# RWKV-6 time mixing with a BitNet feed-forward: decay totals computed first, queries prepared a level ahead, small matmuls split over parts of the array, head variances with the means as stationary operand

## The chip, the cores and the metric

The kernel runs on one core of a Trainium2 chip. Time is device time in microseconds (us). Three runs of the kernel before have a median of 3308.46 us (3307.17 to 3309.01). Engines: PE is TensorE, DVE VectorE, ACT ScalarE, POOL GpSimd, SP SyncE; psP, psW, psX, psY, psF are PSUM tensors.

## The reference, cut to what matters

Input x is 4 x 2048 x 512. An RWKV-6 time mix (16 heads of 32 channels) is followed by a layer norm, a feed-forward with ternary weights (512 to 2048 to 512), and another layer norm:

```python
mix = jnp.tanh((x + xx * time_maa_x) @ maa_w1).reshape(b, t, 5, E_MIX)      # five mixes of rank 32
mix = jnp.einsum('btfe,fec->fbtc', mix, maa_w2); mw, mk, mv, mr, mg = mix
xw = x + xx * (time_maa_w + mw)                                             # and xk, xv, xr, xg likewise
r = xr @ Wr.T; k = xk @ Wk.T; v = xv @ Wv.T; g = jax.nn.silu(xg @ Wg.T)
w = time_decay + jnp.tanh(xw @ td_w1) @ td_w2
decay = jnp.exp(-jnp.exp(w))
def step(S, inp):
    kv = k_t[..., :, None] * v_t[..., None, :]
    y = jnp.einsum('bhk,bhkj->bhj', r_t, S + u[None, :, :, None] * kv)
    S = d_t[..., None] * S + kv
y = ((y - mu) / jnp.sqrt(var + EPS)).reshape(b, t, c) * ln_g + ln_b         # mean and variance per head
x = layernorm(x + (y * g) @ Wo.T)
x = layernorm(x + layernorm(gelu(x @ ternary(W_fc).T)) @ ternary(W_proj).T)
```

## The kernel before

**Tiles.** A tile is 64 time steps of all four batch rows, so 256 columns (`COLS`); `PAIRS` = 2 halves of 128 columns belong to two batch rows each. There are 32 tiles, one after the other, since the state S goes from tile to tile. In tile `it` the attention of tile `it` is interleaved by hand with the feed-forward of tile `it - 1` (`ffn.up`, `ffn.down`, `ffn.stats`, and `ffn.late`, which finishes the tile before that one). Tile 0 has no feed-forward; a last piece (`alone`) has no attention. Each engine runs its own instruction list in program order, and semaphores tie the lists together. `Ring` hands out PSUM banks in a fixed order: `wait_free` waits until the former content of a bank has been read.

**Scan by levels.** Inside a tile the recurrence is solved by doubling: blocks of 1, 2, 4, 8, 16 and 32 steps. `D` holds the decay of each step, `TOT[2n]` the product of decays over 2n steps. At each level DVE multiplies the right halves of the queries `RM` by the total of the left neighbour (`scale_right`, L1114), and the left halves of the keys `KM` by the total of the right neighbour (`scale_left`, L1126), and makes the next total (L1127). Then ACT (three heads of a group, L661) and DVE (the fourth, `queries`, L1102) copy the right query halves into one of two buffers `RB`, PE multiplies keys by queries (`l2`, `l4`, `l8`, `l16` in psW, L464; `l32` at L481), and DVE copies the blocks into `A` (`copy_predicated`, L1169). RM is scaled in place, so `scale_right` of a level waits for the copies of the level below. Between the levels PE runs one `ffn.down(0, i)` each. Before the levels DVE multiplies queries by u (L1138), and PE runs `l1_0` and `l1_1` (L447).

**Order on DVE in the levels.** After `ffn.up(0, 3)`: for n = 2, 4, 8, 16: `scale_right` and `queries` (n = 2 had its own ahead of the loop), `scale_left` with the next total, `copy_predicated`, and at n = 2 `ffn.fold(0, 0)` (L1296), a reduction of 1.0 us.

**After the levels.** ACT copies the blocks into AB (`matrices`), PE makes y (`from_state`, `from_chunk`, L506 and L518), DVE copies it to YSB, ACT squares it (L771). PE sums the squares per head (`var`, L564: eight matmuls with the squares as stationary operand and 4 columns of HEAD_MEAN moving), runs `up(1, 3)` and `down(1, 0)` to `down(1, 2)`. ACT takes square roots (L787) behind its part of `up(1, 3)`, DVE takes reciprocals (L1213) and spreads them over the head's channels (L1217), PE transposes them (`rb`, L577), DVE multiplies y by them, applies the affine map and the gate (L1223 to L1231), and PE runs `wo` (L591). Between `rb` and `wo` PE makes the arguments of the five tanh (`tanh_argument`, L359): `w1a` with 128 columns of stationary operand, `w1b` with 32, each over 256 moving columns. ACT takes their tanh (L792, L794), copies high parts (`mix_high`, L661), POOL the remainders (`mix_low`, L867).

**Start of a tile.** `mix` of "mk" (L375), `td1` (L402, 64 columns stationary), `ffn.late` (`down(before, 1, 3)`, L637), `mix` of "mv", `td2` (L412, 64 rows), `ffn.tokens` (L607), then the k channels (L393), `up(0, 0)` (L618), and so on. ACT takes the tanh of td1 (L684) and the exponentials of td2 (L694). DVE reads the feed-forward's sums in `moments` (L1306). In `F_SEQ` the product of the second half, `pj_1`, stands ahead of its sums, `st_1`, though PE issues the sums first; so `moments` waits for both.

Of the kernel before, what the change touches and what calls it, by code (L numbers as in the profile page):

```python
# [11 lines left out]
ALU = mybir.AluOpType  # L12
# [29 lines left out]
         ("r0", "act"), ("r1", "act"), ("g0", "dve"), ("g1", "dve"), ("var", "act"), ("rb0", "dve"), ("rb1", "dve"),  # L42
# [12 lines left out]
         for n, e in (("fc0", "act"), ("fc1", "act"), ("fc2", "act"), ("fc3", "act"), ("pj", "product"), ("st", "stats"))]  # L55

F_BANKS = [0, 1, 0, 1, 0, 1, 1, 0, 1, 0, 1, 0]
# [47 lines left out]
def rwkv_ffn_kernel(nc, x_ch, x_tok, w_all, w1, w2a, w2b, td1, td2, par, wfc, wpj, ffn_wb, c_f32, c_mask, out,  # L105
                    tiles=TILES):
    with ExitStack() as ctx:
# [11 lines left out]
        TD2 = sb("TD2", [DECR, C])[:, :]  # L119
# [12 lines left out]
        HEAD_MEAN = CF[:, o:o + HPG]; o += HPG  # L132
# [29 lines left out]
        TZ = sb("TZ", [DECR, COLS])[:, :]  # L162
# [61 lines left out]
        rs_inv, y_affine, z_ready = sem("rs_inv"), sem("y_affine"), sem("z_ready")  # L224
        bn_done, mv_ready, rstd_ready = sem("bn_done"), sem("mv_ready"), sem("rstd_ready")
# [37 lines left out]
        NWEIGHTS = 7 + 5 * 4  # L263
# [15 lines left out]
        def _(sp):  # L279
# [49 lines left out]
        def _(pe):  # L329
# [49 lines left out]
            pe.wait_ge(w2_split, 6)  # L379
            mix(-1, 0, "mw", lambda name: None)  # L380

            def tile(it, first, ffn):
# [18 lines left out]
                for k in range(KC):  # L401
                    mm = pe.matmul(psP[0:DECR, P.bank("td1"), 0:COLS], TD1[:, k, :], cc(XF[1], k),  # L402
                                   start=(k == 0), stop=(k == KC - 1))
# [5 lines left out]
                for g in range(2):  # L409
                    P.wait_free(pe, it, f"td2{g}", first)  # L410
                    for c in range(2):
                        mm = pe.matmul(psP[:, P.bank(f"td2{g}"), COLS * c:COLS * (c + 1)],  # L412
                                       TD2[:, 128 * (2 * g + c):128 * (2 * g + c + 1)], TZ[:, :], start=True, stop=True)
                    mm.then_inc(p_full, 1)
# [146 lines left out]
                for p in range(PAIRS):  # L561
                    for c in range(KC):
                        o = HEADS * p + HPG * c
                        mm = pe.matmul(psP[:, P.bank("var"), o:o + HPG], cc(YSQ, c)[:, 128 * p:128 * (p + 1)], HEAD_MEAN,  # L564
                                       start=True, stop=True, skip_group_check=True)
# [33 lines left out]
            def feed_forward(j, before):  # L599
# [41 lines left out]
                def alone():  # L641
                    late()
                    tokens()
                    for p in range(PAIRS):
                        for g in range(4):
                            up(p, g)
                        for part in range(4):
                            down(j, p, part)
                        stats(p)
# [9 lines left out]
        def _(act):  # L659
# [3 lines left out]
            def mix_high(t):  # L663

# [761 lines left out]
```

## Time and profile before

| | |
|---|---|
| median of three runs | 3308.46 us |
| the profiled execution | 3307.6 us, its span 3305.7 us |
| PE busy | 3080.0 us, 93% |
| PE weight load busy | 2229.9 us, 67% |
| DVE busy | 2449.2 us, 74% |
| ACT busy | 1913.6 us, 58% |
| POOL busy | 933.9 us, 28% |
| mean granted PE clock | 0.982 |

Shares are means over stages with different limits; busy time of a matmul is modelled with its end, and matmuls overlap. A row of the timeline gives start, duration, engine, line, operation, output and input, count, and in brackets the idle time of the engine before it with what ended it. A float32 matmul stands in two records.

### The profile page before, as it was taken

What the parts mean: (1) busy time and instruction counts of PE and PEld (TensorE: products, weight loads), DVE (VectorE), ACT (ScalarE), POOL (GpSimd) and SP (SyncE); (2) the same over time, 40 slices, a digit from 0 to 9 for tenths busy, and PEclk for the clock granted to TensorE, in tenths of its full rate; (3) what the DMA queues carried; (4) which work ended last, traced back from release to release, by engine and by line L of the source; (5) the groups of instructions that cost most, each with busy time, mean ns of one, the idle gap of its engine ahead of it and who ended that gap; (6) DMA issues with size and microseconds to landing.
All of it is one profiled execution on the core that took longest, in us unless ns stands there. A gap on an engine that the chain in (4) does not pass through costs nothing.

```text
span 3305.7 us, 98915 instructions
## 1 busy us (share of the span) xinstructions
PE 3080.0 (93%) x39133; PEld 2229.9 (67%) x39133; DVE 2449.2 (74%) x5172; ACT 1913.6 (58%) x3919; POOL 933.9 (28%) x825
## 2 busy tenths in 40 slices
PE   1899999999999999999999999999999999999997
PEld 0667666767666767666767666767666767666765
DVE  8467787777787777787777687777777777787777
ACT  0456566556566556566655566655566655566654
POOL 3223322223322223322233322233322233322232
PEclk9899999999999999999999999999999999999999
DMA  5000000000000000000000000000000000000000
GB/s 198 14 8 21 15 18 21 18 14 21 15 18 21 18 14 21 16 17 21 18 14 21 20 13 21 18 15 20 21 12 21 18 16 19 21 12 21 18 21 14
DMA packets 22741, 73.24 MB, mean 22 GB/s; under 512 B 3088, under 2 KB 3344, under 8 KB 20688
## 3 DMA queue, kind: packets, MB, share of 16 engines
q1 hardware_dynamic: 22352, 66.96, 5.9%
q8 instruction: 378, 6.19, 0.8%
q14 instruction: 11, 0.09, 0.0%
HBM read 50.17 MB, written 16.78 MB: 20 GB/s over the span
## 4 chain that ended last, share of the span: by engine, by line
PE 48%; DVE 27%; ACT 13%; issue 10%; DVEq 1%; DMA 1%; ACTq 0%; POOL 0%; SPq 0%; POOLq 0%
PE psP L393 10%; PE psP L425 7%; PE psF L637 5%; PE psP L591 5%; ACT HHI L820 4%; PE psF L618 4%; DVE HLO L1288 4%; ACT ARENA L661 3%; DVE ARENA L1138 3%; ACT GG L811 2%; DVE SUMS L1280 2%; DVE ARENA L1126 2%; PE psW L464 2%; PE psW L481 2%; DVE ARENA L1169 2%
## 5 line engine op out<-in xcount | busy, mean ns | idle before, releaser
L661 ACT ACTIVATE ARENA<-ARENA 32x512 f32<-32x512 f32 (+3 forms) x1026 | 581.1, 569 | 263.9 <-DVE ARENA L1114 202.1
L393 PE MATMUL psP<-ARENA,WALL 128*128 128x256 f32 x3072 | 688.0, 380 | 0.2 <-ACT ARENA L694 0.2
L393 PEld LDWEIGHTS psP<-ARENA,WALL 128*128 128x128 f32 x3072 | 574.4, 190 | 73.7 <-issue 0.7
L1288 DVE SCALAR_TENSOR_TENSOR HLO<-GG,FWB,HHI 128x128 f16<-128x128 f32 x1024 | 302.0, 357 | 368.1 <-ACT HHI L820 362.9
L618 PE MATMUL psF<-XHI,WFC 128*128 128x128 f16 x4096 | 487.0, 220 | 2.4 <-DVE ST L1306 2.1
L618 PE MATMUL psF<-XLO,WFC 128*128 128x128 f16 x4096 | 485.7, 219 | 0.0
L618 PEld LDWEIGHTS psF<-XHI,WFC 128*128 128x128 f16 x4096 | 400.4, 99 | 31.5 <-issue 26.3
L881 POOL TENSOR_TENSOR ARENA<-ARENA,XT 128x1024 f32<-128x1024 f32 x128 | 278.2, 2174 | 505.5 <-DVE ARENA L1059 505.5
L618 PEld LDWEIGHTS psF<-XLO,WFC 128*128 128x128 f16 x4096 | 401.4, 98 | 17.6 <-issue 10.3
L637 PE MATMUL psF<-WPJ,HHI 128*128 128x512 f16 x1024 | 405.7, 396 | 4.7 <-ACT GG L811 4.7
L637 PE MATMUL psF<-WPJ,HLO 128*128 128x512 f16 x1024 | 402.3, 393 | 0.0
L820 ACT ACTIVATE HHI<-GG,FWB 128x128 f16<-128x128 f32 x1024 | 327.4, 390 | 25.3
L874 POOL TENSOR_TENSOR FV<-FV,CF 128x1 f32<-128x1 f32 x64 | 43.1, 673 | 1022.7 <-DVE FV L1312 1022.7
L867 POOL TENSOR_TENSOR MT<-ARENA 32x256 fp32r<-32x256 f32 x330 | 297.4, 901 | 107.0 <-ACT ARENA L661 83.7
L1059 DVE SCALAR_TENSOR_TENSOR ARENA<-psX,PAR,XX 128x256 f32<-128x256 f32 x322 | 140.2, 476 | 200.2 <-PE psX L375 191.1
L811 ACT ACTIVATE GG<-psF 128x512 f32<-128x512 f32 x256 | 151.7, 593 | 218.0 <-PE psP L393 136.2
L591 PE MATMUL psP<-WALL,ARENA 128*128 128x512 f32 x512 | 233.5, 599 | 2.8 <-DVE ARENA L1231 0.2
L425 PE MATMUL psP<-WALL,ARENA 128*128 128x512 f32 x512 | 224.9, 592 | 0.0
L464 PE MATMUL psW<-ARENA 128*32 128x64 f32 x8192 | 154.4, 232 | 71.2 <-ACT ARENA L661 63.4
L464 PEld LDWEIGHTS psW<-ARENA 128*32 128x32 f32 x8192 | 131.9, 117 | 125.4 <-ACT ARENA L661 82.1
L637 PEld LDWEIGHTS psF<-WPJ,HHI 128*128 128x128 f16 x1024 | 103.2, 101 | 138.0 <-issue 37.1
L661 ACT ACTIVATE ARENA<-psP 128x256 f32<-128x256 f32 (+1 forms) x192 | 93.5, 525 | 154.8 <-PE psP L393 154.8
(164 smaller groups left out, 5298.9 us busy)
## 6 DMA issues: line engine op xcount, KB each, us to landing
XT<-x_ch SPq DMA_DIRECT2D x33, 520.0 KB, 3.4
ARENA<-x_tok SPq DMA_DIRECT2D x32, 512.0 KB, 4.8
out<-OUT SPq DMA_DIRECT2D x64, 256.0 KB, 3.0
WALL<-w_all SPq DMA_DIRECT2D x5, 1024.0 KB, 15.9
ARENA<-wfc SPq DMA_DIRECT2D x4, 1024.0 KB, 8.0
ARENA<-wpj SPq DMA_DIRECT2D x3, 1024.0 KB, 14.8
GG<-wpj SPq DMA_DIRECT2D x1, 1024.0 KB, 18.8
OUT<-w2a SPq DMA_DIRECT2D x8, 64.0 KB, 15.2
```

Source lines behind the costliest of these rows:

```text
L393: mm = pe.matmul(psP[:, P.bank(f"{name}{g}"), COLS * c:COLS * (c + 1)], WALL[:, w, k, 128 * (2 * g + c):128 * (2 * g + c + 1)], cc(XF[slot ...
L425: mm = pe.matmul(psP[:, P.bank(f"v{p}"), :], cc(XF[1], k)[:, 128 * p:128 * (p + 1)], WALL[:, W_V, k, :], start=(k == 0), stop=(k == KC - 1))
L464: mm = pe.matmul(psW[BLK * (q % 4):BLK * (q % 4 + 1), W.bank(name), o:o + 64], cc(KM, c)[:, BLK * q:BLK * (q + 1)], RB[RB_SEQ[name]][:, c, ...
L591: mm = pe.matmul(psP[:, P.bank(f"wo{p}"), :], cc(YSB, k)[:, 128 * p:128 * (p + 1)], WALL[:, W_O, k, :], start=(k == 0), stop=(k == KC - 1))
L618: mm = pe.matmul(psF[:, F.bank(name), 128 * m:128 * (m + 1)], WFC[:, k, 128 * (4 * g + m):128 * (4 * g + m + 1)], x[:, p, k, :], start=(k ...
L637: mm = pe.matmul(psF[:, F.bank(f"pj_{p}"), :], h[:, m, :], WPJ[:, m, :], start=(m == 0 and h is HHI), stop=(m == MH - 1 and h is HLO))
L661: return act.activation(o, i, ACT.Copy)
L811: act.activation(GG[:, u % 2, 0, :], psF[:, F.bank(f"fc{g}_{p}"), :], ACT.Gelu).then_inc(f_act, 1)
L820: e = act.activation(HHI[:, k, :], GG[:, u % 2, 0, 128 * m:128 * (m + 1)], ACT.Copy, scale=FWB[:, 0, k:k + 1])
L867: pool.tensor_tensor(MT[f][rows(1 + 2 * (n % 2)), :], whole, high, ALU.subtract).then_inc(mt_low, 1)
L881: pool.tensor_tensor(v, v, xcur, ALU.add).then_inc(xf_ready, 1)
L1288: e = dve.scalar_tensor_tensor(out=HLO[:, k, :], in0=GG[:, u % 2, 0, 128 * m:128 * (m + 1)], scalar=FWB[:, 0, k:k + 1], in1=HHI[:, k, :], ...
```

## The change

1. `totals()`: all six decay totals are made on DVE in one chain, ahead of the multiplication of the queries by u. `scale_left` no longer makes them.
2. In the levels, `scale_right` and `queries` run one level ahead: in round i, `scale_right(i + 2)`, `scale_left(i + 1)`, `queries(i + 2)`, then `copy_predicated`. `fold(0, 0)` moves from n = 2 to n = 4.
3. `td1`: eight matmuls over 128 columns each, the two column halves in two halves of the array's columns, instead of four over 256. `td2`: eight matmuls, the column halves in two halves of the array's rows. TD2 is held twice. The exponentials of td2 become eight over 128 columns.
4. `w1b`: sixteen matmuls over 64 columns in four column groups, instead of four over 256; its tanh becomes four of 32 x 64. ACT makes the high part of the first mix before that tanh.
5. `var`: HEAD_MEAN (32 columns) is the stationary operand and the squares move: four matmuls over 256 columns in four column groups. The root is taken over 128 x 256 into D, two transposes put the result into psP, and DVE takes the reciprocal from there. ACT's root stands ahead of its `up(1, 3)`; PE's transposes stand between `down(1, 1)` and `down(1, 2)`.
6. `st_1` comes ahead of `pj_1` in `F_SEQ`.

```diff
-         ("r0", "act"), ("r1", "act"), ("g0", "dve"), ("g1", "dve"), ("var", "act"), ("rb0", "dve"), ("rb1", "dve"),
+         ("r0", "act"), ("r1", "act"), ("g0", "dve"), ("g1", "dve"), ("var", "dve"), ("rb0", "dve"), ("rb1", "dve"),
...
-         for n, e in (("fc0", "act"), ("fc1", "act"), ("fc2", "act"), ("fc3", "act"), ("pj", "product"), ("st", "stats"))]
+         for n, e in (("fc0", "act"), ("fc1", "act"), ("fc2", "act"), ("fc3", "act"))
+         + ((("pj", "product"), ("st", "stats")) if p == 0 else (("st", "stats"), ("pj", "product")))]
...
                 for k in range(KC):
-                    mm = pe.matmul(psP[0:DECR, P.bank("td1"), 0:COLS], TD1[:, k, :], cc(XF[1], k), ...)
+                    for h in range(2):
+                        mm = pe.matmul(psP[DECR * h:DECR * (h + 1), P.bank("td1"), 0:128], TD1[:, k, :], cc(XF[1], k)[:, 128 * h:128 * (h + 1)], ...)
...
+                for c in range(KC):
+                    for h in range(2):
+                        r = slice(DECR * h, DECR * (h + 1))
+                        mm = pe.matmul(psP[:, P.bank(f"td2{h}"), 128 * c:128 * (c + 1)], TD2[r, 128 * c:128 * (c + 1)], TZ[r, :],
+                                       start=True, stop=True)
...
+                        for q in range(4):
+                            mm = pe.matmul(ps[MIXR * q:MIXR * (q + 1), 0:CH], W1[:, k, 4 * MIXR:5 * MIXR],
+                                           cc(XF[1], k)[:, CH * q:CH * (q + 1)], ...)
...
-                for p in range(PAIRS):
-                    for c in range(KC):
-                        o = HEADS * p + HPG * c
-                        mm = pe.matmul(psP[:, P.bank("var"), o:o + HPG], cc(YSQ, c)[:, 128 * p:128 * (p + 1)], HEAD_MEAN, ...)
+                for c in range(KC):
+                    mm = pe.matmul(psP[HD * c:HD * (c + 1), P.bank("var"), 0:COLS], HEAD_MEAN, cc(YSQ, c), ...)
                 mm.then_inc(p_full, 1)
                 if ffn:
                     ffn.up(1, 3)
                     ffn.down(1, 0)
                     ffn.down(1, 1)
+                pe.wait_ge(deviations, it + 1)
+                for p in range(PAIRS):
+                    mm = pe.transpose(psP[:, P.bank("var"), COLS + 128 * p:COLS + 128 * (p + 1)], D[:, 128 * p:128 * (p + 1)], IDENT)
+                mm.then_inc(turned, 1)
+                if ffn:
                     ffn.down(1, 2)
-                pe.wait_ge(rs_inv, 2 * it + 2)
+                pe.wait_ge(rs_inv, it + 1)
...
                 if ffn:
-                    for g in range(1, 4):
-                        ffn.up(1, g)
+                    ffn.up(1, 1)
+                    ffn.up(1, 2)
                 act.wait_ge(p_full, P.full(it, "var"))
-                act.activation(RS[:, :, :, :], psP[:, P.bank("var"), 0:PAIRS * HEADS]..., ACT.Sqrt, bias=EPS[:, 0:1]).then_inc(p_act, 1)
+                act.activation(D[:, 0:COLS], psP[:, P.bank("var"), 0:COLS], ACT.Sqrt, bias=EPS[:, 0:1]).then_inc(deviations, 1)
+                if ffn:
+                    ffn.up(1, 3)
...
+                def totals():
+
+                    for i in range(NPL):
+                        t = TOT[2 ** i].rearrange("p (q two) -> p two q", two=2)
+                        if i:
+                            dve.wait_ge(tot_ready, NPL * it + i)
+                        dve.tensor_tensor(TOT[2 ** (i + 1)], t[:, 0, :], t[:, 1, :], ALU.mult).then_inc(tot_ready, 1)
...
                     dve.tensor_tensor(left, left, grow(tr, n), ALU.mult).then_inc(k_scaled, 1)
-                    dve.tensor_tensor(TOT[2 * n], tl, tr, ALU.mult).then_inc(tot_ready, 1)
-                    dve.wait_ge(tot_ready, NPL * it + i + 1)
-                    dve.wait_ge(r_scaled, NPL * it + i + 1)
-                    dve.wait_ge(k_scaled, NPL * it + i + 1)
...
+                dve.wait_ge(d_ready, it + 1)
+                totals()
                 dve.wait_ge(p_act, P.read(it, "r1"))
...
                 scale_right(1, 2)
+                queries(1, 4)
                 if ffn:
                     ffn.up(0, 3)
                 for i, n in enumerate(LEVELS):
-                    if i:
-                        scale_right(i + 1, n)
+                    scale_right(i + 2, 2 * n)
                     scale_left(i + 1, n)
+                    if i + 2 < NPL - 1:
+                        queries(i + 2, 4 * n)
...
-                    if ffn and n == 2:
+                    if ffn and n == 4:
                         ffn.fold(0, 0)
-                scale_right(5, 32)
...
-                dve.wait_ge(p_act, P.read(it, "var"))
-                dve.reciprocal(RS[:, :, :, :], RS[:, :, :, :]).then_inc(rs_inv, 1)
+                dve.wait_ge(turned, it + 1)
+                dve.reciprocal(RS[:, :, :, :], psP[:, P.bank("var"), COLS:2 * COLS]...[:, :, :, 0:HPG]).then_inc(p_dve, 1)
```

## Rows read from the trace of the kernel before

**Rows 1.** The page: busy time of each engine over the span.
```profile
PE 3080.0 (93%) x39133; PEld 2229.9 (67%) x39133; DVE 2449.2 (74%) x5172; ACT 1913.6 (58%) x3919; POOL 933.9 (28%) x825
```
**Rows 2.** Windows (busy of PE, PEld, DVE, ACT, POOL; clock): two tiles, DVE's stretch.
```profile
1669.03:1768.00 98.97, 95.36 (x1221) 69.35 (x1220) 73.97 (x161) 59.48 (x122) 27.88 (x26) 0.98 0.06 18
...
2164.25:2262.03 97.78, 93.97 (x1221) 68.41 (x1220) 74.10 (x160) 59.51 (x122) 27.87 (x26) 1.00 0.06 18
...
1704.45:1730.80 26.35, 24.27 (x426) 17.16 (x423) 23.71 (x50) 18.24 (x36) 0.00 (x0) 0.94 0.01 2
```
**Rows 3.** Timeline of PE in the levels of one tile: l8, l32.
```profile
1723.59 1.93 PE L464 MATMUL psW<-ARENA 128*32 128x64 f32 x64 [2.08 <-ACT ARENA L661]
...
1730.92 1.94 PE L481 MATMUL psW<-ARENA 128*32 128x128 f32 x32
```
**Rows 4.** The same tile of rows 6's last row: l8 on PE.
```profile
2218.84 1.10 PE L464 MATMUL psW<-ARENA 128*32 128x64 f32 x64 [2.12 <-ACT ARENA L661]
```
**Rows 5.** Timeline of ACT, same tile: queries of l8, then matrices(0).
```profile
1721.63 1.91 ACT L661 ACTIVATE ARENA<-ARENA 32x512 f32<-32x512 f32 x3 [4.22 <-DVE ARENA L1114]
...
1730.82 2.55 ACT L661 ACTIVATE ARENA<-ARENA 32x512 f32<-32x512 f32 x4 [0.79 <-DVE ARENA L1169]
```
**Rows 6.** Timeline of DVE, same tile: u product, levels; last row another tile.
```profile
1704.45 3.45 DVE L1138 TENSOR_TENSOR ARENA<-ARENA,PAR 32x256 f32<-32x256 f32 x8
...
1720.91 0.68 DVE L1114 TENSOR_TENSOR ARENA<-ARENA,TOT 128x512 f32<-128x512 f32 x1
...
1730.08 0.71 DVE L1169 COPY_PREDICATED ARENA<-CM,psW 128x512 f32<-128x512 uint32 x1
...
2224.14 0.71 DVE L1169 COPY_PREDICATED ARENA<-CM,psW 128x512 f32<-128x512 uint32 x1
```
**Rows 7.** Timeline of PE: rb and wo.
```profile
1755.70 1.09 PE L577 MATMUL psP<-CF,ARENA 128*128 128x128 f32 x8 [0.27 <-DVE ARENA L1217]
...
1760.45 3.70 PE L591 MATMUL psP<-WALL,ARENA 128*128 128x512 f32 x8
```
**Rows 8.** Timeline of DVE: from the variances to the gated output.
```profile
1752.25 1.67 DVE L1047 SCALAR_TENSOR_TENSOR ARENA<-XX,PAR,XT 128x256 f32<-128x256 f32 x4
1754.57 0.35 DVE L1213 RECIPROCAL RS<-RS 128x32 f32<-128x32 f32 x1 [0.65 <-ACT RS L787]
...
1759.71 0.69 DVE L1231 TENSOR_TENSOR ARENA<-ARENA 128x512 f32<-128x512 f32 x1
```
**Rows 9.** Start of the tile: DVE moments, then PE's k channels.
```profile
1674.48 0.16 DVE L1306 TENSOR_SCALAR ST<-psF 128x2 f32<-128x2 f32 x1 [0.31 <-PE psF L637]
...
1677.72 7.07 PE L393 MATMUL psP<-ARENA,WALL 128*128 128x256 f32 x32
```
**Rows 10.** Windows with line L1127 alone: the totals of a tile.
```profile
1669.03:1768.00 98.97, 1.96 (x6) 0.98 0.06 18
```
**Rows 11.** The levels on DVE, the tile followed: `scale_left` of l8 and l16.
```profile
1725.57 0.69 DVE L1126 TENSOR_TENSOR ARENA<-ARENA,TOT 128x512 f32<-128x512 f32 x1 [0.50 <-PE psW L464]
...
1729.23 0.69 DVE L1126 TENSOR_TENSOR ARENA<-ARENA,TOT 128x512 f32<-128x512 f32 x1 [0.75 <-PE psW L464]
```
**Rows 12.** Groups by form on PE: busy us, mean ns of one.
```profile
L447 PE MATMUL psW<-ARENA 128*32 128x128 f32 x2048 | 62.7, 274 | 0.0
L564 PE MATMUL psP<-CF,ARENA 128*128 128x4 f32 x512 | 62.5, 254 | 0.0
```
**Rows 13.** Timeline of ACT: root and tanh with their table loads.
```profile
1752.95 1.28 ACT L787 ACT_TABLE_LOAD   x1
...
1754.55 1.28 ACT L792 ACT_TABLE_LOAD   x1
1758.56 0.38 ACT L792 ACTIVATE ARENA<-psX 128x256 f32<-128x256 f32 x1 [2.73 <-PE psX L359]
```
**Rows 14.** Group of the exponentials on ACT: busy us, mean ns | idle before.
```profile
L694 ACT ACTIVATE ARENA<-psP,PAR 128x256 f32<-128x256 f32 x128 | 53.6, 470 | 96.2 <-PE psP L412 95.4
```
**Rows 15.** Tile 0, PE in the levels: l16.
```profile
146.07 1.93 PE L464 MATMUL psW<-ARENA 128*32 128x64 f32 x64 [0.91 <-DVE ARENA L1126]
```

More of the change, by code:

```diff
@@ L408, in tile @@
                 pe.wait_ge(p_act, P.read(it, "td1"))
[L409 to L414, printed above, removed]
+                for h in range(2):
+                    P.wait_free(pe, it, f"td2{h}", first)
+                for c in range(KC):
+                    for h in range(2):
+                        r = slice(DECR * h, DECR * (h + 1))
+                        mm = pe.matmul(psP[:, P.bank(f"td2{h}"), 128 * c:128 * (c + 1)], TD2[r, 128 * c:128 * (c + 1)], TZ[r, :],
+                                       start=True, stop=True)
+                        if c == KC - 1:
+                            mm.then_inc(p_full, 1)
                 if ffn:
@@ L661, in copy, with high, mix_high @@
                 return act.activation(o, i, ACT.Copy)
-            def mix_high(t):
+            def high(t, f):
+                src = TMA[rows(f), :] if f < 4 else TMB
+                copy(MT[f][rows(0), :], src)
+                copy(MT[f][rows(2), :], src).then_inc(mt_high, 1)
+            def mix_high(t, arguments, n):
+                act.wait_ge(tm_ready, M.read(t, "w1a"))
+                copy(TMH.bitcast(F32R), TMA[:, :]).then_inc(tm_rounded, 1)
+                high(t, 0)
+                act.wait_ge(arguments, n)
+                ps = M_BANKS[M.bank("w1b")]
+                for q in range(4):
+                    e = act.activation(TMB[:, CH * q:CH * (q + 1)], ps[MIXR * q:MIXR * (q + 1), 0:CH], ACT.Tanh)
+                e.then_inc(tm_ready, 1)
+                for f in range(1, 4):
+                    high(t, f)
                 act.wait_ge(tm_ready, M.read(t, "w1b"))
-                copy(TMH.bitcast(F32R), TMA[:, :]).then_inc(tm_rounded, 1)
                 copy(TMBH.bitcast(F32R), TMB[:, :]).then_inc(tm_rounded, 1)
-                for f in range(5):
-                    src = TMA[rows(f), :] if f < 4 else TMB
-                    copy(MT[f][rows(0), :], src)
-                    copy(MT[f][rows(2), :], src).then_inc(mt_high, 1)
+                high(t, 4)
             act.wait_ge(su_dve, 6)
@@ L691, in tile @@
                     act.wait_ge(p_full, P.full(it, f"td2{g}"))
-                    for c in range(2):
-                        k = 2 * g + c
-                        e = act.activation(cc(D, k), psP[:, P.bank(f"td2{g}"), COLS * c:COLS * (c + 1)], ACT.Exp,
+                    for k in range(KC):
+                        e = act.activation(cc(D, k)[:, 128 * g:128 * (g + 1)], psP[:, P.bank(f"td2{g}"), 128 * k:128 * (k + 1)], ACT.Exp,
                                            bias=PAR[:, k, DECAY:DECAY + 1])
@@ L792, in tile @@
                 act.activation(TMA[:, :], M_BANKS[M.bank("w1a")][:, 0:COLS], ACT.Tanh).then_inc(tm_ready, 1)
[L793 to L795 removed]
+                mix_high(it, m_full, M.full(it, "w1b"))
             def feed_forward(j, before):
```

80 lines of the change are left out of this document (43 added, 37 removed).

## Prediction

> **What bounds the kernel now.** I read the page first: PE is busy 93% of the span, DVE 74% [rows 1]. That looks like a PE-bound kernel, in which PE work taken out is time taken out. The windows of single tiles correct this: the tile that I follow takes 98.97 us at clock 0.98, another 97.78 us at clock 1.00 [rows 2]. 31 tiles have a feed-forward, so they are nearly the whole span. Both tiles have the same one large wait of PE, for ACT's query copies ahead of l8, 2.08 and 2.12 us; behind it the same 64 records of l8 take 1.93 us in the one and 1.10 in the other [rows 3, 4]. In most tiles PE falls to 1.2 GHz behind the wait, in some it stays at 2.4.
>
> Then I looked at who makes PE wait. ACT's queries of l8 start at 1721.63 after 4.22 us without work, released by DVE's `scale_right` of 1720.91 [rows 5, 6]. DVE is busy 23.71 of the 26.35 us from 1704.45 to 1730.80 [rows 2]. So in the levels DVE is the bound and PE waits for it. The stretch ends with the last `copy_predicated`, 1730.08 + 0.71 = 1730.79; it releases ACT's `matrices(0)` at 1730.82 [rows 5, 6], and from there ACT and DVE carry the chain through y, squares and roots until `rb` at 1755.70, for which PE waits 0.27 us [rows 7]. Then DVE works without a pause to its half of the gate, done at 1759.71 + 0.69 = 1760.40; `wo` starts at 1760.45 [rows 7, 8]. DVE then makes the next tile's inputs. Only from the k channels, 1677.72 [rows 9], to 1704.45 does PE alone set the pace, and there the change removes nothing. I follow the tile by its anchors: last `copy_predicated`, `rb`, `wo`, k channels.
>
> **Parts 1 and 2, totals and levels.** Nothing is taken from DVE: the six totals are 1.96 us wherever they stand [rows 10]. Ahead of the u product each waits for the one before, some 0.2 us in all: 2.16 us. So the u product, 3.45 us from 1704.45 [rows 6], ends at 1710.05, and PE's `l1_1`, which needs it, waits; I estimate 0.7 us. In the loop a `scale_right` now stands ahead of the `scale_left` on which the next product waits: l4 waits about 1.0 us for it (1.5 us of totals and 0.7 of `scale_right` more are ahead of it, of which PE's own wait takes up some). Then the look-ahead pays: l8's queries are copied while `down` and l4 run, and l8 goes without a wait. What sets the anchor is DVE's list. Of its 26.35 us, 0.50 and 0.75 are waits for l8 and l16, which the half clock made late [rows 11]; they go, since `scale_right` of the next level now fills them. The sixth total (0.2) comes inside, and the waits in the chain of totals (0.2). 26.35 - 1.25 + 0.4 = 25.5: the last copy ends at about 1730.0, 0.8 us earlier.
>
> The other tile bounds this from below. At full clock its last copy ends 2224.14 + 0.71 - 2218.84 = 6.01 us behind l8's start, against 1730.79 - 1723.59 = 7.20 [rows 3, 4, 6]: the clock alone is worth 1.2 us, and against such a tile the new order is 0.4 us slower. Bounds: 0.4 worse, if the clock stays as it is, to 3.5 better, if DVE followed and PE's wait and the clock were both saved in full (2.08, and about 1.6 of work at half clock). I take the value by DVE's row.
>
> **Part 5, variances and roots.** PE's sixteen `var` records are 62.5 / 32 = 1.95 us a tile. Of float32 records in four column groups the trace has 64 of 128 columns in 62.7 / 32 = 1.96 us [rows 12]; eight of 256 columns are a quarter of that, 0.5 us. Two transposes cost half of `rb`'s 1.09 [rows 7]. But `rb` hangs on DVE. ACT's `up(1,3)` takes about 2.45 us ahead of the root's load at 1752.95 [rows 13]. Without it the load starts at 1750.5, the root (0.47 with a bias [rows 14]) ends at 1752.25, as PE leaves `down(1,1)`, and the transposes end at 1752.95. DVE's `mixed_by_x` runs from 1752.25 to 1753.92 anyway; the reciprocal, which waited 0.65 us for the root [rows 8], follows at once, at 1753.96 for 1754.57. Gain 0.6 us, whatever `var` costs PE up to its old 1.95; below, 0 if the transposes come late.
>
> Here a rule speaks against the edit. The root's load starts right behind ACT's last work and takes 1.28 us [rows 13]. The Trainium skill (ScalarE: Activation LUTs, "What ACT_TABLE_LOAD costs") gives a switch 1283 ns and another 1380 ns of drain, and under "Table sets" asks to batch calls by set, while here Gelu, Sqrt and Gelu alternate. By its drain the root would end at 1753.6, the reciprocal would start at about 1754.4, and the gain would be 0.2 for 0.6; the trace shows the load, and no drain beside it.
>
> The loads are now: Sqrt, Gelu, none for the tanh of w1a (today's tanh behind the Gelus needs none), and one ahead of Exp, so four a tile for three. Is the new one exposed? The load of L792 stands ahead of the wait of its own instruction: loaded at 1754.55, tanh at 1758.56 after a wait of 2.73 us [rows 13]. Ahead of Exp ACT idles 96.2 / 32 = 3.0 us, for td2 [rows 14]. If the load lies ahead of that wait too, it costs 0; otherwise up to 1.3 us. I take 0, by L792.
>
> **Part 4, w1b.** Some 1.9 us on PE become 0.5. But `wo` waits for the gate, 1760.45 - 1755.70 = 4.75 us behind `rb` [rows 7]. PE then waits about 1.4 us: gain 0. ACT and POOL begin the mixes up to 3 us earlier, into slack. DVE's part of `up(1,3)` is queued behind the gate, which covers ACT's `up(1,3)` being 3 us later; without that cover DVE's list to the next tile would be late by it.
>
> **Parts 3 and 6, start of the tile.** `moments` waits 0.31 us for `pj_1` [rows 9]; that goes. td1 and td2 cost PE about 1.9 us each, half of it if two halves of the array overlap as four column groups do. `mix` of "mv" must wait until DVE has read "mk", so td1's gain is mostly lost; td2's reaches the tokens, which wait for DVE's normalised rows, 0.3 earlier. The eight small exponentials free the first bank about 1.25 us behind td2, as the tokens end. The k channels gain 0.35 us beyond the 0.6; bounds 0 (nothing overlaps) and 1.8 (both halves in full).
>
> The second TD2 load lies in the setup under the quantising of weights: 0.
>
> **Sum.** 0.8 + 0.6 + 0.35 = 1.75 us a tile; 31 tiles: 54 us, and tile 0 perhaps 1. The profiled execution took 3307.6 us, 0.03% under the median: 3307.6 - 55 = about 3253 us, 1.7% faster. The measurement can tell 0.2%, 6.6 us, from no change.
>
> **The rivals.**
> - *PE's work pays in full.* If DVE and ACT have slack where I see none: 0.9 for var, 1.4 for w1b, 1.8 for td1 and td2, 3.5 for the wait and its clock make 7.6 us a tile, 3072 us; half of that, 3190. For it: PE's 93% [rows 1]. Against: DVE's unbroken rows. 15%.
> - *The half clock moves, or table loads show.* The waits of 1.0 ahead of l4 and 1.4 ahead of `wo` drop the clock as 2.08 did [rows 3]; the 0.27 ahead of `rb` did not. A drop costs PE some 1.7 us, and DVE's bound hides about two thirds: 0.6 each, 1.2 in all, 3290 us. Exp's load exposed, 1.3 a tile, gives 3293. 20%.
> - *Slower: the clock stays down through the levels.* In tile 0, l16 takes 1.93 us behind a wait of only 0.91 [rows 15]: with one wait after the other half clock holds. The waits ahead of l1, l4 and l16 (0.7, 1.0, 0.5) could do that in every tile. From l4 to l32 PE has some 8.3 us of work in 9.1; at half clock 16.6, so 7.5 later, less the 1.75: 5.7 a tile, 3485 us. It decides where the half-clock stretch passes some 7 us. Over all this side 10%.
> - *No change.* The totals' delay cancels the gains: 3308 us. 5%.
>
> **How the numbers follow.** Forecast 50%, more gain 15%, less gain 20%, same 5%, slower 10%. The forecast's own range is 3205 to 3275; a good half of "more gain" lies above 3185, the lesser gains end at 3300, "same" at about 3310. 3185 to 3308 holds 8 in 10. Faster 0.85, same 0.05, slower 0.10.
>
> **What would show it.** Levels: PE's 2 us wait ahead of l8 gone, about 1 us ahead of l4 for `scale_left`, DVE nearly unbroken from the totals on, l8 records of 1.10 us, clock 0.99. Roots: no wait of the reciprocal for ACT. `wo`: PE waits 1 to 1.5 us for L1231's counterpart. ACT: four table loads, that of Exp ahead of its wait. PE's busy time falls by more than the span. I am wrong if PE waits less than 1 us ahead of `wo` (DVE had slack), or if half clock shows in new places.

## The result, and the profile after

The changed kernel takes 3356.94 us (median of 4 runs, 3352.3 to 3357.68), beside 3308.74 us for the kernel before in the same measurement (4 runs, 3307.17 to 3309.09). The ratio is 1.0144, 95% interval 1.0126 to 1.0161: slower by 1.4%, 48 us. The forecast was 3253, with a range that ended at 3308. It was wrong in sign.

The page's first row, of after, against [rows 1]: PE's busy time fell by 117 us, DVE's rose by 73, the span grew by 50. The granted clock is 0.984 for 0.982.

```profile
PE 2962.8 (88%) x40245; PEld 2156.6 (64%) x40245; DVE 2522.0 (75%) x5172; ACT 1993.1 (59%) x4175; POOL 912.6 (27%) x825
```

A tile's period is 100.78 us after, 99.02 before (means over tiles 3 to 29). The table measures anchors from the start of the last addition of the next tile's decay input (L1101, before L1070), in the same tiles:

| anchor, us from that addition | before | after | difference |
|---|---|---|---|
| k channels begin (PE) | 8.70 | 8.74 | +0.04 |
| last `copy_predicated` ends (DVE) | 61.53 | 62.04 | +0.51 |
| reciprocal begins (DVE) | 85.59 | 85.76 | +0.17 |
| `rb` begins (PE) | 86.72 | 86.91 | +0.19 |
| gated output ends (DVE) | 91.42 | 91.61 | +0.19 |
| low parts of `up(1, 3)` end (DVE) | 92.47 | 94.23 | +1.76 |
| the period | 99.02 | 100.78 | +1.76 |

Up to the gate the tile lost 0.19 us, where 1.75 were to be gained. Then 1.57 are lost within four instructions of DVE (L1323, `HLO`: the low parts of the feed-forward's outputs), and none of it comes back. Here they are, in the timeline of DVE of the kernel after:

```profile
1781.32 0.69 DVE L1266 TENSOR_TENSOR ARENA<-ARENA 128x512 f32<-128x512 f32 x1
1781.93 2.70 DVE L1323 SCALAR_TENSOR_TENSOR HLO<-GG,FWB,HHI 128x128 f16<-128x128 f32 x4
1784.56 1.21 DVE L1315 TENSOR_TENSOR SUMS<-SUMS,GG 128x1024 f32<-128x1024 f32 x1
1785.81 2.00 DVE L1331 TENSOR_REDUCE GR<-SUMS 128x128 f32<-128x512 f32 x2
...
1791.18 1.23 DVE L1101 TENSOR_TENSOR ARENA<-ARENA,XT 128x1024 f32<-128x1024 f32 x1
```

POOL in the same stretch of after, with its first and fourth product of the mixes (`mix_low`, L898) alone and then all ten:

```profile
1782.17 0.72 POOL L898 TENSOR_TENSOR MT<-ARENA 32x256 fp32r<-32x256 f32 x1 [1.36 <-DVE ARENA L1266]
1784.56 1.80 POOL L898 TENSOR_TENSOR MT<-ARENA 32x256 fp32r<-32x256 f32 x1
...
1782.17 7.48 POOL L898 TENSOR_TENSOR MT<-ARENA 32x256 fp32r<-32x256 f32 x8 [1.36 <-DVE ARENA L1266]
1789.81 1.51 POOL L898 TENSOR_TENSOR MT<-ARENA 32x256 fp32r<-32x256 f32 x2 [0.16 <-POOL MT L898]
```

And the same places of the kernel before, DVE and POOL, which stand in no group ahead of the prediction:

```profile
1760.32 1.14 DVE L1288 SCALAR_TENSOR_TENSOR HLO<-GG,FWB,HHI 128x128 f16<-128x128 f32 x4
...
1762.62 2.00 DVE L1296 TENSOR_REDUCE GR<-SUMS 128x128 f32<-128x512 f32 x2
...
1761.61 9.80 POOL L867 TENSOR_TENSOR MT<-ARENA 32x256 fp32r<-32x256 f32 x10 [2.41 <-ACT ARENA L661]
```

Before, POOL waited for ACT's tanh of w1b and began at 1761.61, when DVE's group had just ended (1760.32 + 1.14 = 1761.46). After, ACT makes the first high part ahead of that tanh and w1b itself is shorter, so POOL waits only for DVE's gated output (L1266). It begins at 1782.17, 0.24 us into the group, and the group takes 2.70 us for 1.14. From the gate to the next tile's decay input DVE's list has no gap in either kernel. So the 1.56 us are the tile's.

PE shows what follows, in the timeline of after:

```profile
1789.52 0.50 PE L644 MATMUL psF<-CF,GR 128*128 128x1 f32 x4
1792.01 0.49 PE L384 MATMUL psX<-MT,W2S 128*128 128x256 f32 x2 [2.00 <-POOL MT L898]
...
1792.67 1.73 PE L413 MATMUL psP<-ARENA,TD 128*64 128x128 f32 x16
```

PE now waits 2.00 us ahead of "mk". The view names POOL, whose last product ends at 1791.32; but "mk" starts 0.7 us behind that, and by the kernel it waits only for the fourth product. PE's sequencer takes its sums only when DVE's folds are done, and the branch at the end of the loop then holds it for 3.68 us (from 1787.96; before, 3.67 us from 1764.77). Behind the wait td1 takes 1.73 us in this tile and 1.09 in the one before it: here too the clock falls to 1.2 GHz behind some of the waits.

### The profile page after: what moved, and what is told of

Its sections match the earlier page's. It is cut to its first block, busy times and chain, and to the rows that moved or that the text cites. A ratio compares the mean times of both kernels' runs of the same rounds, so it can differ in the third digit from the quotient of the medians.

```text
span 3355.6 us, 101584 instructions
## 1 busy us (share of the span) xinstructions
PE 2962.8 (88%) x40245; PEld 2156.6 (64%) x40245; DVE 2522.0 (75%) x5172; ACT 1993.1 (59%) x4175; POOL 912.6 (27%) x825
## 4 chain that ended last, share of the span: by engine, by line
DVE 41%; PE 31%; issue 16%; ACT 9%; DVEq 1%; POOL 1%; DMA 1%; ACTq 0%; SPq 0%; POOLq 0%
PE psP L403 10%; DVE HLO L1323 7%; PE psP L439 7%; PE psF L635 5%; ACT ARENA L681 5%; DVE SUMS L1315 3%; DVE ARENA L1205 3%; DVE ARENA L1090 3%; DVE ARENA L1171 3%; ACT HHI L849 2%; DVE SUMS L1312 2%; DVE ARENA L1151 2%; PE psY L532 2%; DVE TOT L1141 2%; DVE X L1296 2%
## 5 line engine op out<-in xcount | busy, mean ns | idle before, releaser
L1323 DVE SCALAR_TENSOR_TENSOR HLO<-GG,FWB,HHI 128x128 f16<-128x128 f32 x1024 | 356.4, 409 | 368.1 <-ACT HHI L849 362.9
L898 POOL TENSOR_TENSOR MT<-ARENA 32x256 fp32r<-32x256 f32 x330 | 274.7, 833 | 74.1 <-DVE ARENA L1266 42.0
L478 PE MATMUL psW<-ARENA 128*32 128x64 f32 x8192 | 142.6, 222 | 71.8 <-DVE ARENA L1162 69.3
L478 PEld LDWEIGHTS psW<-ARENA 128*32 128x32 f32 x8192 | 124.5, 111 | 126.1 <-issue 126.1
L608 PEld LDWEIGHTS psP<-WALL,ARENA 128*128 128x128 f32 x512 | 92.2, 189 | 139.1 <-issue 91.9
```

The lines of the kernel that those rows point to most:

```text
L478: mm = pe.matmul(psW[BLK * (q % 4):BLK * (q % 4 + 1), W.bank(name), o:o + 64], cc(KM, c)[:, BLK * q:BLK * (q + 1)], RB[RB_SEQ[name]][:, c, ...
L608: mm = pe.matmul(psP[:, P.bank(f"wo{p}"), :], cc(YSB, k)[:, 128 * p:128 * (p + 1)], WALL[:, W_O, k, :], start=(k == 0), stop=(k == KC - 1))
L898: pool.tensor_tensor(MT[f][rows(1 + 2 * (n % 2)), :], whole, high, ALU.subtract).then_inc(mt_low, 1)
L1323: e = dve.scalar_tensor_tensor(out=HLO[:, k, :], in0=GG[:, u % 2, 0, 128 * m:128 * (m + 1)], scalar=FWB[:, 0, k:k + 1], in1=HHI[:, k, :], ...
```

## The experiments

Each ratio is to the kernel before, with its 95% interval. Anchors are means over tiles 3 to 29.

**POOL waits for the outputs' low parts.** The changed kernel with one wait on POOL ahead of `mix_low`:

```diff
+                if ffn:
+                    ffn.cleared()
...
+                def cleared():
+                    pool.wait_ge(hlo_ready, 8 * j + 8)
```

> The changed kernel, with one wait more: POOL begins the remainders of the mixes (mix_low) only when DVE has done its scalar_tensor_tensor of up(1,3). Theory A (DVE's four instructions of up(1,3) take 2.70 us for 1.14 because POOL works beside them, and DVE's list to the next tile is unbroken, so 1.57 us a tile are lost): they fall back to about 1.14 us, the tile from 100.8 to about 99.2 us, the kernel by 31 x 1.57 = 49 us to about 3308 us, no more than 0.2% from the kernel before. Theory B (the loss is PE's: its longer instruction list makes it wait ahead of the state's matmuls, 31.7 us over the span): nothing changes, 3357 us. Theory C (PE's wait for POOL's remainders at the start of the tile, 56.3 us, is the loss): POOL later by 1.2 us makes it worse, 3390 us.

Measured: 3312.16 us (10 runs), ratio 1.0012 [1.0, 1.0024]; 45 us come back. DVE, POOL and PE of this kernel:

```profile
1761.09 1.14 DVE L1328 SCALAR_TENSOR_TENSOR HLO<-GG,FWB,HHI 128x128 f16<-128x128 f32 x4
...
1762.38 8.20 POOL L898 TENSOR_TENSOR MT<-ARENA 32x256 fp32r<-32x256 f32 x8 [2.41 <-DVE HLO L1328]
...
1769.67 0.50 PE L384 MATMUL psX<-MT,W2S 128*128 128x256 f32 x2 [0.30 <-issue]
...
1770.34 1.09 PE L413 MATMUL psP<-ARENA,TD 128*64 128x128 f32 x16
```

The group is back at 1.14 us, the wait ahead of "mk" is 0.30 and td1 is at full clock, as theory A had it. The loss is the overlap of POOL with DVE, and the rest of the change is worth nothing: that is the second miss, 55 us of forecast gain that aren't there.

**The early start alone.** The kernel before, with ACT's and POOL's mixes in the new order and nothing else:

```diff
+                high(t, 0)
+                act.wait_ge(arguments, n)
+                act.activation(TMB[:, :], M_BANKS[M.bank("w1b")][0:MIXR, 0:COLS], ACT.Tanh).then_inc(tm_ready, 1)
...
-                pool.wait_ge(tm_rounded, 2 * t + 4)
+                pool.wait_ge(tm_rounded, 2 * t + 3)
...
+                    if n == 8:
+                        pool.wait_ge(tm_rounded, 2 * t + 4)
```

> The kernel before, with one part of the change alone: ACT makes the high part of the first mix ahead of the tanh of w1b, and POOL begins the remainders behind it, so up to 2 us earlier. Theory A: DVE's up(1,3) now meets POOL there too and takes 2.3 to 2.7 us for 1.14; the tile gets 1.2 to 1.6 us longer, the kernel 3345 to 3357 us. Theories B and C: no change or slightly faster, 3300 to 3309 us, since PE's list is as before and the remainders are earlier.

Measured: 3401.57 us, ratio 1.0288 [1.0271, 1.0306], 94 us slower. That is theory A's sign, but twice its size. From the gate to the low parts' end a tile loses 1.57 us, as in the change. Another 1.15 are lost at the start of the next tile, where the k channels begin 9.85 us behind the anchor for 8.70; td1 is the old one there, of half-filled columns. DVE, POOL and PE of this kernel:

```profile
1801.18 2.70 DVE L1294 SCALAR_TENSOR_TENSOR HLO<-GG,FWB,HHI 128x128 f16<-128x128 f32 x4
...
1801.42 7.48 POOL L873 TENSOR_TENSOR MT<-ARENA 32x256 fp32r<-32x256 f32 x8 [1.36 <-DVE ARENA L1237]
...
1811.04 0.50 PE L375 MATMUL psX<-MT,W2S 128*128 128x256 f32 x2 [1.78 <-POOL MT L873]
...
1811.79 2.87 PE L403 MATMUL psP<-ARENA,TD 128*64 128x256 f32 x8
```

td1 takes 2.87 us here, and the granted clock of the span is 0.969. So the early start costs the same 1.57 us in either kernel. In the changed kernel the lower clock delays nothing (k channels at 8.74), and I take it that the shorter td1 and td2 absorb it; no run separates that.

**The levels undone, with and without POOL's wait.** Parts 1 and 2 taken back (`totals` gone, `scale_right`, `queries` and `fold(0, 0)` where they were), first in the changed kernel, then in that with POOL's wait:

```diff
-                totals()
...
-                    scale_right(i + 2, 2 * n)
+                    if i:
+                        scale_right(i + 1, n)
```

> The changed kernel with parts 1 and 2 undone: totals between the levels, queries not ahead, fold at n = 2. My prediction gave these parts 0.8 us a tile; then this runs 25 us slower than the changed kernel, 3382 us. The traces of the two kernels show the stretch from up(0,1) to the last masked copy at 28.6 us before and 29.0 after, so DVE sets it in both orders: then 3345 to 3357 us, the same within 0.3%, with the 2 us wait ahead of l8 back.

> The changed kernel with POOL waiting for DVE's up(1,3), as in e1_pool_waits, and the totals and levels as before the change. e1_pool_waits ran at 3312 us; e3_levels_undone was 7 us faster than the changed kernel. If the new order of the levels costs time on DVE (its stretch from up(0,1) to the last masked copy took 28.45 us undone and 29.0 us in the changed kernel), this runs 7 to 15 us faster than e1_pool_waits: 3297 to 3305 us. If the new order pays the 0.8 us a tile of my prediction: 3337 us.

Measured: 3350.09 us, ratio 1.0124 [1.0107, 1.0141]; and 3297.45 us, ratio 0.9969 [0.9957, 0.9981]. Beside the kernels with the new order that is 7 us, with intervals that overlap, and 15 us, clear of them: with POOL's wait the new order costs time. In the profiled executions of that pair the last copy ends at the same place (61.96 and 61.98) and `rb` begins 0.33 us earlier with the old order, where PE's stall in `values` (below) is 20.8 us over the span for 29.1. So part of the 15 us may be the stall and not the order; no run separates them. Parts 3 to 6 with POOL's wait are together worth 10 us.

**td1 and td2 undone.** The changed kernel with the old td1, td2 and exponentials:

```diff
-                    for h in range(2):
-                        mm = pe.matmul(psP[DECR * h:DECR * (h + 1), P.bank("td1"), 0:128], ...)
+                    mm = pe.matmul(psP[0:DECR, P.bank("td1"), 0:COLS], TD1[:, k, :], cc(XF[1], k), ...)
```

> The changed kernel with part 3 undone: td1 and td2 again four matmuls over 256 columns each, four exponentials. The prediction gave this part 0.35 us a tile with the wait of moments, most of it not from the matmuls: then 3357 to 3365 us. If PE's work counts in full, 1.7 us a tile: 3410 us. PE's instruction list is 32 matmul and load records a tile shorter: if the wait ahead of the state's matmuls comes from where the list is refilled, it moves or shrinks here, and the chain to rb gets up to 0.8 us shorter, 3335 us.

Measured: 3362.12 us, ratio 1.016 [1.0143, 1.0177], 5 us above the change, with intervals that overlap. Whether part 3 is worth anything by itself stays unclear: the k channels begin 0.79 us later (9.53), but `rb` at the same place (86.89). PE's waits in this kernel:

```profile
PE psX L384 <- POOL MT L895: 54.4, 27, 2.3
...
PE psF L631 <- issue: 27.2, 31, 1.1
```

The second row is new: PE idles 27.2 us, 31 times, within `up`, "issue" being a wait for nothing that the profile shows, where the changed kernel had a like stall in `values` (below). There it has none, and the way from the last copy to `rb` is 24.30 us for 24.87.

**The roots undone.** With POOL's wait, and part 5 taken back:

```diff
-                act.activation(D[:, 0:COLS], psP[:, P.bank("var"), 0:COLS], ACT.Sqrt, ...).then_inc(deviations, 1)
-                if ffn:
-                    ffn.up(1, 3)
```

> The changed kernel with POOL waiting as in e1_pool_waits, and the variances and roots as before the change (eight matmuls with the squares stationary, root behind up(1,3) on ACT, reciprocal from SBUF). My prediction gave the part 0.6 us a tile: then 3312 + 19 = 3331 us. By the trace of the changed kernel the way from the last masked copy to rb is 0.3 us shorter than before, since PE now waits up to 1.2 us within the state's matmuls and DVE's sums come later: if that wait is a matter of where PE's list is refilled, it moves with the longer list here, and the result may lie anywhere from 3300 to 3331 us.

Measured: 3317.98 us, ratio 1.0036 [1.0022, 1.0049]. Part 5 is worth 6 us by the medians, 0.2 a tile; the intervals just touch. The stall in `values` is 18.3 us here for 29.1, so the 6 us are what part 5 leaves after it.

**The sixth `scale_right` behind the last copy.** Counting DVE's instructions in the levels showed one more than before. The kernel with POOL's wait, and this one moved back:

```diff
-                    scale_right(i + 2, 2 * n)
+                    if i + 2 < NPL - 1:
+                        scale_right(i + 2, 2 * n)
...
+                scale_right(5, 32)
                 if ffn:
                     ffn.fold(0, 1)
```

> e1_pool_waits with one DVE instruction moved: the sixth scale_right (that of 32 steps, 0.69 us) goes from ahead of the last two products of the levels to behind the last copy_predicated, where the kernel before has it. DVE's stretch from its first instruction of the levels to the end of the last copy held five scale_rights before (3.45 us) and holds six now (4.13 us), and took 26.34 and 26.33 us. Theory A (the missing gain of the levels is this instruction): the last copy ends 0.6 to 0.9 us earlier; of that 0.5 to 0.8 us a tile comes through, 3288 to 3297 us for e1's 3312. Theory B (the gain is lost in the waits of PE for scale_left or in the stalls of PE behind): the copy comes 0.6 us earlier and the tile stays, 3308 to 3314 us. Theory C (the products of the next stage wait for the moved instruction): slower than e1.

Measured: 3301.9 us (9 runs, 3292.55 to 3309.44), ratio 0.9979 [0.9967, 0.9991]. DVE of this kernel at the end of the levels:

```profile
1720.67 0.71 DVE L1211 COPY_PREDICATED ARENA<-CM,psW 128x512 f32<-128x512 uint32 x1
...
1721.61 0.69 DVE L1156 TENSOR_TENSOR ARENA<-ARENA,TOT 128x512 f32<-128x512 f32 x1 [0.22 <-DVE ARENA L1211]
```

The last copy ends 0.62 us earlier than with POOL's wait alone (61.36 for 61.98), as theory A had it, but `rb` begins only 0.23 earlier, and the period is 98.82 for 99.06. So A holds for the anchor, and 0.4 of it is lost behind, as B had it; the time lies between the two forecasts.

**The last sums in DVE's idle time.** In the kernel before DVE waits 5.41 us ahead of the "mr" inputs. The kernel with POOL's wait and the levels undone, with the last addition of the squares, both folds, the moments and PE's stats product of the second half put there. With them three more things move: `F_SEQ` has the old order (part 6 undone), PE makes the mix of "mr" ahead of `up(0, 0)`, and POOL's `ffn.late` stands one mix later. No run separates these from the sums.

```diff
-                    ffn.up(1, 3)
-                    ffn.fold(1, 0)
-                    ffn.fold(1, 1)
+                    ffn.up(1, 3, False)
...
                     ffn.tokens()
+                    ffn.late_sums()
+                    ffn.moments()
+                    ffn.late()
```

> e6_pool_waits_levels_undone with DVE's last addition and the two folds of the feed-forward's second half, moments and PE's stats(1) moved out of the stretch between the gate and the next tile's k channels, into the 5.4 us in which DVE has nothing to do ahead of mr. If DVE sets that stretch, the tile loses 0.6 to 1.6 us and the kernel 20 to 50 us: 3250 to 3285 us, faster than both kernels. If PE sets it, nothing changes, 3300 us. PE's wait for L1271's counterpart ahead of wo stays.

> e5_sums_later without POOL's wait for the outputs of half a tile: POOL starts its first product of the mixes at the gate's product again, beside DVE's group of four products of the outputs. Theory A (the shared port costs time only because DVE's list from the gate to the next tile's decay input had no gap): here DVE has a gap ahead of the mixes' ends, so the group takes about 2.7 us for 1.1 but the tile grows by less than half of that: 3280 to 3300 us. Theory B (the contention is paid in full wherever DVE stands): 1.5 us a tile over e5, about 3329 us. Theory C (POOL's earlier results let PE begin the mixes sooner and that pays something back): below 3280 us.

> The kernel before with one thing moved: the last sums of the second half (DVE's add, two folds and the moments, PE's stats product) go behind DVE's products of the outputs, into the idle time ahead of the mixes' ends. If DVE's list from the gate to the next tile sets the tile, 0.6 to 1.0 us a tile: 3275 to 3290 us, and with the 10 us that the change's later parts gave in e6 it adds up to e5's 3280. If e5's gain needed the totals' new order in the gate and the queries ahead, nothing: 3300 to 3312 us. A rival: the stats product comes to stand in PE's list behind a wait and DVE's gain is lost again, 3310 us or more.

> e10 and the later sums of e5 together: the new order of the levels with the sixth scale_right behind the last copy, POOL's wait for the outputs, and DVE's last sums of the second half in its idle time at the start of the next tile. e5 has the same with the old order of the levels and took 3280 us. If the new order pays once that instruction is out of it: 3262 to 3278 us. If the new order is worth nothing beside the old one at its best: 3278 to 3285 us. If PE's waits for scale_left ahead of l4, l8 and l16 cost more than ACT's copies ahead of l8 did: above 3285 us.

Measured, in this order: 3279.86 us, ratio 0.9911 [0.9896, 0.9926], the fastest version here; 3291.3 us, 0.9951 [0.9938, 0.9965]; 3293.89 us, 0.9951 [0.9937, 0.9964]; 3282.48 us, 0.992 [0.9906, 0.9933]. DVE with POOL's wait (the first):

```profile
1748.79 1.13 DVE L1323 SCALAR_TENSOR_TENSOR HLO<-GG,FWB,HHI 128x128 f16<-128x128 f32 x4
1749.84 0.54 DVE L1380 TENSOR_SCALAR OUT<-OUT,FMV,OSD 128x512 f32<-128x512 f32 x1
1752.67 0.69 DVE L1278 TENSOR_TENSOR X<-psP,ARENA 128x512 f32<-128x512 f32 x1 [2.29 <-PE psP L609]
```

and without it (the second):

```profile
1750.82 2.70 DVE L1318 SCALAR_TENSOR_TENSOR HLO<-GG,FWB,HHI 128x128 f16<-128x128 f32 x4
1753.45 1.01 DVE L1375 TENSOR_SCALAR OUT<-OUT,FMV,OSD 128x512 f32<-128x512 f32 x1
1754.70 0.69 DVE L1273 TENSOR_TENSOR X<-psP,ARENA 128x512 f32<-128x512 f32 x1 [0.24 <-PE psP L609]
...
1757.71 1.70 DVE L1101 TENSOR_TENSOR ARENA<-ARENA,XT 128x1024 f32<-128x1024 f32 x1
```

In both DVE waits for `wo`. With that gap POOL's early start still stretches the group to 2.70 us, the next instruction to 1.01, and the decay input's addition to 1.70, but it costs 11 us for the 45 that it cost without a gap: theory A. The gap takes up what lies ahead of it. The 0.47 us on the addition lie behind it: td1 begins 0.46 us later than with POOL's wait (mean over the tiles), and 0.22 of that is left in the period (98.24 for 98.02). The sums later alone gave 15 us on the kernel before, less than the 18 to 33 forecast, and 18 on the one with the change's parts 3 to 6. With the sums moved, the new order of the levels without its sixth `scale_right` and the old order are equal (3282.48 and 3279.86, with overlapping intervals).

## Why the prediction was wrong

**The step that failed** is the sentence in part 4: "ACT and POOL begin the mixes up to 3 us earlier, into slack." They do begin earlier, and POOL's own results have slack. But POOL's start isn't free for DVE. DVE's four short products lie where POOL now works, and that list of DVE was the bound, as the prediction had said of the stretch ahead of it. The earlier start was priced as a result that nobody needed, not as work that now runs beside other work. It is 1.57 us a tile by the anchors and 45 us by the run without the overlap, which is at 3312. None of the rivals named it. The forecast of part 4 itself held: PE waits 1.36 us ahead of `wo`, for the 1.4 predicted, and w1b's PE time gained nothing. PE's rows of after, against [rows 7]:

```profile
1780.06 0.65 PE L366 MATMUL psY<-ARENA,W 128*32 128x64 f32 x32
1782.07 3.70 PE L608 MATMUL psP<-WALL,ARENA 128*128 128x512 f32 x8 [1.36 <-DVE ARENA L1266]
```

`wo` takes 3.70 us behind this wait, as before, so the clock didn't fall there. The half clock did show in one new place, td1 behind the 2.00 us ahead of "mk", which the prediction had named as a sign of being wrong.

The Trainium skill has the rule (SBUF — State Buffer, section "SBUF: two separate sides"): VectorE and GpSimd share a port pair, and it is an exclusive lock. A GpSimd instruction, or a VectorE instruction in a two-port mode, or one with two inputs in SBUF if the GpSimd instruction reads SBUF, has it for the whole instruction if it starts first; the other waits in full. The trace agrees, by its 2.70 for 1.14 us; the prediction had not weighed it.

**Levels: 0.8 predicted, 0.5 lost.** The mechanism came as forecast: ACT's copies are there in time and l8 takes 1.10 us. PE in the levels of after, against [rows 3, 4]:

```profile
1742.02 1.10 PE L478 MATMUL psW<-ARENA 128*32 128x64 f32 x64 [0.98 <-DVE ARENA L1162]
1745.43 1.10 PE L478 MATMUL psW<-ARENA 128*32 128x64 f32 x64 [0.48 <-DVE ARENA L1162]
1749.09 1.10 PE L478 MATMUL psW<-ARENA 128*32 128x64 f32 x64 [0.73 <-DVE ARENA L1162]
```

The waits are 0.98 ahead of l4 (about 1.0 predicted), 0.48 and 0.73 ahead of l8 and l16, and all three products run at full clock: the rival by which the clock stays down is refuted. But DVE's stretch isn't shorter, and DVE sets the anchor. Here are windows with `scale_right` alone, of before and of after, from DVE's first instruction that the change touches to the end of the last copy:

```profile
1704.45:1730.79 26.34, 3.45 (x5) 0.94 0.01 2
```
```profile
1725.99:1752.32 26.33, 4.13 (x6) 1.00 0.01 2
```

My sum said 26.35 - 1.25 + 0.4 = 25.5, for 26.33 measured. It left out a term: looking ahead by a level brings the sixth `scale_right`, 0.69 us, ahead of the last copy, where the kernel before had it behind. 25.5 + 0.69 = 26.2; the last 0.1 us I can't assign. Moving it back took 0.62 us off at the anchor: in that kernel the stretch is 25.7 us in every tile, near the 25.5 of the sum. The second half of the miss was in the bounds: against a tile at full clock the new order was to be 0.4 worse. In the kernel with the levels undone DVE's stretch takes 1748.83 - 1723.66 = 25.17 us in a tile of full clock, and 26.33 is 1.16 worse, about the 0.4 and the sixth `scale_right` together:

```profile
1723.66 3.44 DVE L1169 TENSOR_TENSOR ARENA<-ARENA,PAR 32x256 f32<-32x256 f32 x8
...
1748.10 0.73 DVE L1200 COPY_PREDICATED ARENA<-CM,psW 128x512 f32<-128x512 uint32 x1
```

The tile that the prediction followed is the common one, but not the only one. Of tiles 3 to 29 before, 21 take 26.3 or 26.4 us for this stretch and 6 take 25.2, a mean of 26.10. After, every tile takes 26.3. So the stretch itself lost 0.22 of the 0.51 us, and the other 0.29 are lost ahead of it, where the prediction had the change do nothing. Most of that is the same overlap in a second place: before `up(0, 1)`'s sums DVE has another group of four low parts, and POOL's addition of the bias (L962, before L931) runs beside its start. The group takes 1.44 us in the mean before and 1.64 after. POOL now waits in 13 tiles for an output store to land, 0.46 us in the one shown, so it reaches further into the group; before, it did so once. Why the stores land later no run tested. POOL and DVE of after:

```profile
1520.16 2.50 POOL L962 TENSOR_TENSOR OUT<-X,BSUM 128x512 f32<-128x512 f32 x2 [0.46 <-DMA out<-OUT]
```
```profile
1521.64 1.96 DVE L1323 SCALAR_TENSOR_TENSOR HLO<-GG,FWB,HHI 128x128 f16<-128x128 f32 x4 [4.20 <-ACT HHI L849]
```

**Roots: 0.6 predicted, 0.3 at `rb`, 0.2 in the time.** The stretch from the last copy to `rb` is 24.87 us for 25.19. The steps were right. ACT's load and root, PE's transposes and `rb`, DVE's reciprocal, in after, against [rows 8, 13]:

```profile
1772.90 1.28 ACT L817 ACT_TABLE_LOAD   x1
1774.20 0.47 ACT L817 ACTIVATE ARENA<-psP,CF 128x256 f32<-128x256 f32 x1
1774.69 1.28 ACT L840 ACT_TABLE_LOAD   x1
```
```profile
1774.99 0.38 PE L585 MATMUL psP<-CF,ARENA 128*128 128x128 f32 x2
...
1777.31 1.09 PE L594 MATMUL psP<-CF,ARENA 128*128 128x128 f32 x8 [0.20 <-DVE ARENA L1252]
```
```profile
1776.17 0.35 DVE L1248 RECIPROCAL RS<-psP 128x32 f32<-128x32 f32 x1
```

The load stands 0.02 us behind ACT's last work and the root 0.02 behind the load, so no drain beside the load took the gain; the reciprocal follows DVE's products without a wait. What ate the gain lies ahead of it: PE stalls within `values` (L560), its products of keys and values for the state.

```profile
1767.03 0.23 PE L560 MATMUL psY<-V,ARENA 64*32 64x32 f32 x3 [1.24 <-issue]
```

In the list of PE's waits this is 31.7 us in 31 times, for 7.9 at the same line before; `values` takes 2.48 us for 1.72 (means). By its place it moves with PE's list: with td1 and td2 undone it is `up` that stalls. In that kernel `values` has no stall and the stretch from the last copy to `rb` is 24.30 us, 0.9 less than before, where the changed kernel gains 0.3. In the trace the instruction queue's DMA brings a piece just ahead of the stall (1764.63 to 1765.52 in this tile; PE goes on at 1767.03). That PE ran out of instructions is argued from this, not shown; no run tested it.

**Start of the tile: 0.35 predicted, 0 measured.** td1 takes 1.09 us at full clock (1.55 in the mean, the clock having fallen in some tiles) and td2 1.16, for the predicted half of 1.9. But the tokens wait for DVE. PE, DVE and POOL of after, against [rows 9]:

```profile
1696.20 1.16 PE L425 MATMUL psP<-TZ,TD 64*128 64x128 f32 x16
1698.31 1.11 PE L624 MATMUL psW<-CF,X 128*128 128x128 f32 x8 [0.95 <-DVE X L1296]
```
```profile
1696.38 2.33 DVE L1296 TENSOR_SCALAR X<-X,MV,RSTD 128x512 f32<-128x512 f32 x2
```
```profile
1695.79 2.18 POOL L912 TENSOR_TENSOR ARENA<-ARENA,XT 128x1024 f32<-128x1024 f32 x1 [1.39 <-DVE ARENA L1090]
```

And DVE of the kernel before:

```profile
1675.24 1.93 DVE L1261 TENSOR_SCALAR X<-X,MV,RSTD 128x512 f32<-128x512 f32 x2
```

The gain of the two products became a wait of 0.95 us for DVE's normalised rows. "tokens, which wait for DVE's normalised rows, 0.3 earlier" named the bound, and part 6 did its work: `moments` no longer waits, and DVE begins the rows 0.28 us earlier (5.81 us behind the anchor for 6.09, means). But it ends them at the same place, 8.14 for 8.13. The first of the two takes 1.87 us for 1.58, the second 0.53 in either kernel, and POOL's addition beside the first ends at 7.40 and 7.39. So this gain too went where POOL works beside DVE; that is read from the two traces, no run moved POOL's addition away.

**Exp's table load** is hidden, as taken: it ends at 1694.92 and the first exponential starts at 1697.39, behind a wait for td2.

## What to carry to other kernels

An edit that lets an engine off the bound start earlier is priced by what it will then run beside, not by its slack: look for the bounding engine's instructions in the stretch that it moves into. The same holds for an instruction of the bounding engine that is moved earlier: what it gains can end at its neighbour's end. When a loop looks ahead by one step, write down for the anchor which instructions stand ahead of it before and after, one by one; the look-ahead brings one more of its kind in front of the anchor. And PE time taken from in front of a wait is no gain: of 117 us here at most some 10 arrived, and only with POOL's wait and the old order of the levels.

## What the runs showed of the hardware

- DVE's products with both inputs in SBUF and POOL's take turns, one instruction each: with POOL at work the four of DVE are recorded at 344, 847, 873 and 877 ns for about 350 each (group 1.14 us before), and POOL's stay at 0.72 us. The longer one isn't favoured: POOL's product that starts with DVE's addition of 1.21 us takes 1.80 us, and the addition keeps its 1.21.
- The two folds, reductions that read one tensor, aren't touched: they take 2.00 us with POOL beside them in either kernel, and POOL's products beside them 0.72. DVE's normalising `TENSOR_SCALAR` is: 1.87 us for the one beside POOL's addition, 0.53 for the one that starts behind it. So what a neighbour costs depends on the form of the instruction, and of what stood beside POOL here the group of many short products lost most.
- Matmuls of float32 on parts of the array overlap for the most part: sixteen records of td1 in two column parts take 1.09 us at full clock (1.94 for the eight of twice the columns before), 32 of w1b in four parts 0.65, eight of `var` in four parts 0.64 (1.90 for the sixteen before).
- The branch at the end of PE's loop is recorded at 3.67 and 3.68 us in the tiles followed before and after (3.3 to 4.0 over the loop), and "mk" starts 0.4 us behind its end in both. So what PE waits for ahead of the branch delays the next tile even where PE seems to have 2 us to spare.
